# Cross attention on one core: block 2's first query projection moved in front of the first scores, and mask rows held until a block's maxima have landed

## What is computed

```python
q = split_heads(x @ W_Q.T); k = split_heads(ctx @ W_K.T); v = split_heads(ctx @ W_V.T)
scores = einsum('bhqd,bhkd->bhqk', q, k) / sqrt(16)
scores = where(mask[:, None, :, :] == 1, -1e9, scores)
p = softmax(scores, axis=-1)
concat = merge_heads(einsum('bhqk,bhkd->bhqd', p, v))
out = concat @ W_O.T + x                       # residual
out = (out - mean(out)) * rsqrt(var(out) + 1e-5) * gamma + beta
```

## Time and profile before

| what | value |
|---|---|
| device time, median of 3 runs | 176.94 us (175.6 to 178.7) |
| device time of the profiled execution | 177.09 us |
| its span from the first to the last instruction | 175.3 us |
| busy time of PE in the span | 152.7 us (87%) |
| busy time of DVE | 139.5 us (80%) |
| busy time of ACT | 105.1 us (60%) |
| busy time of POOL | 96.0 us (55%) |
| mean granted clock of TensorE | 0.971 of full speed |

### The profile page before, as it was taken

The page is one execution under the profiler, slowest core; times in us unless marked ns, Lnnn a source line. Parts: engine busy times, 40 slices in busy tenths (PEclk is TensorE's granted clock), DMA queues, the critical chain, the costliest instruction groups (busy, mean ns, idle before and its releaser), DMA issues.

```text
span 175.3 us, 3587 instructions
## 1 busy us (share of the span) xinstructions
PE 152.7 (87%) x1264; PEld 82.4 (47%) x1264; DVE 139.5 (80%) x308; ACT 105.1 (60%) x140; POOL 96.0 (55%) x125
## 2 busy tenths in 40 slices
PE   7699939887969999999999999998899798799840
PEld 7456515344335356345545544563456363164530
DVE  0967743569399969998999899899989975759894
ACT  3123224355377883888877897778576559796400
POOL 8300430010564525337767977974744785899890
PEclk9999985899999999999999999999999999999996
DMA  5959868764867997887498877749460023011206
GB/s 157 382 142 135 242 101 258 230 161 103 268 172 196 286 292 184 222 277 168 137 236 234 247 200 178 214 162 228 133 223 5 0 120 123 2 64 60 120 0 239
DMA packets 21909, 30.24 MB, mean 173 GB/s; under 512 B 3436, under 2 KB 17436, under 8 KB 21892
## 3 DMA queue, kind: packets, MB, share of 16 engines
q1 hardware_dynamic: 20340, 28.18, 56.4%
q10 hardware_dynamic: 1552, 1.84, 3.8%
HBM read 11.28 MB, written 4.19 MB: 88 GB/s over the span
## 4 chain that ended last, share of the span: by engine, by line
PE 51%; DVE 19%; DMA 10%; issue 9%; ACT 5%; POOL 2%; ACTq 1%; SPq 0%; DVEq 0%; POOLq 0%
PE pv_ps L993 12%; PE scores_ps L984 9%; DVE neg_max L725 7%; PE max_ps L951 6%; PE work_ps L924 6%; PE work_ps L930 5%; PE scores_ps L930 4%; DMA R<-neg_max_t 4%; DMA x_t<-in_x_cols 4%; DVE ctx_q L733 3%; PE work_ps L1012 3%; DMA R<-first_max_t 3%; ACT probs L594 2%; PE work_ps L1009 2%; ACT neg_max_t L584 1%
## 5 line engine op out<-in xcount | busy, mean ns | idle before, releaser
L594 ACT ACTIVATE probs<-scores_ps 78x1024 f32<-78x1024 f32 x60 | 60.5, 1016 | 24.4 <-PE scores_ps L984 19.6
L725 DVE TENSOR_REDUCE neg_max<-max_ps 128x6 f16<-128x462 f32 (+1 forms) x84 | 44.7, 560 | 5.2 <-PE max_ps L951 5.1
L951 PEld LDWEIGHTS max_ps<-kb,R 125*128 125x128 f16 x512 | 26.4, 99 | 36.9 <-DVE neg_max L725 21.0
L409 POOL TENSOR_TENSOR ctx_n<-ctx_q,rden 128x256 f32<-128x256 f32 x31 | 19.8, 639 | 43.0 <-DVE rden L735 42.9
L984 PE MATMUL scores_ps<-R,kb 127*78 127x512 f16 x120 | 37.0, 392 | 2.3 <-DMA R<-first_max_t 2.0
L951 PE MATMUL max_ps<-kb,R 125*128 125x77 f16 x512 | 32.5, 201 | 6.1 <-DVE neg_max L725 5.5
L993 PE MATMUL pv_ps<-probs,v_all 78*32 78x512 f32 x248 | 33.0, 604 | 2.6 <-ACT probs L594 1.5
L733 DVE STREAM_TRANSPOSE ctx_q<-pv_ps 128x512 f32<-128x512 f32 x31 | 21.8, 704 | 4.6 <-PE pv_ps L993 4.4
L430 POOL TENSOR_TENSOR y<-y,gamma_sb 128x512 f32<-128x512 f32 x14 | 17.8, 1276 | 2.4 <-ACT y L599 2.4
L392 POOL TENSOR_SCALAR eq<-mask_i 77x512 f16<-77x512 int32 x3 | 5.8, 1928 | 22.1 <-DMA mask_i<-in_mask_cols 22.1
L599 ACT ACTIVATE y<-y,shift,rstd 128x256 f32<-128x256 f32 x28 | 15.1, 591 | 3.6 <-POOL shift L423 3.6
(11 more groups left out here) (105 smaller groups left out, 198.7 us busy)
## 6 DMA issues: line engine op xcount, KB each, us to landing
R<-eq SPq DMA_DIRECT2D x12, 616.0 KB
R<-q SPq DMA_DIRECT2D x46, 128.0 KB
x_t<-in_x_cols SPq DMA_DIRECT2D x8, 512.0 KB, 5.9
y<-in_x SPq DMA_DIRECT2D x8, 512.0 KB, 6.0
out<-y SPq DMA_DIRECT2D x7, 512.0 KB, 2.7
mask_i<-in_mask_cols SPq DMA_DIRECT2D x8, 154.0 KB
out<-y ACTq DMA_DIRECT2D x2, 256.0 KB, 2.1
kb<-k SPq DMA_DIRECT2D x10, 39.0 KB, 3.2
```

Source lines behind the costliest of these rows:

```text
L409: nc.gpsimd.tensor_tensor(ctx_n[:, v, :, u * DK:(u + 1) * DK], ctx_q[:, t % 2, :, 0:DK], rden[:, t % 2, :].unsqueeze(2).to_broadcast([P, C ...
L594: nc.scalar.activation(probs[:, s, :, :], scores_ps[scores_buffer(PAIRS * n + s)[0]][0:COLS, :, :], ACT.Exp).then_inc(exp_done, 1)
L725: nc.vector.tensor_reduce(to[:, t, lo:hi], max_ps[u % 2][:, 0:(hi - lo) * KEYS].rearrange("p (h k) -> p h k", k=KEYS), AX.X, ALU.max, nega ...
L951: last = nc.tensor.matmul(max_ps[u % 2][:, (h - lo) * KEYS:(h - lo + 1) * KEYS], R[m % R_RING][0:MAX_ROW, h, t * P:(t + 1) * P], kb[0:MAX_ ...
```

## The change

Three things are edited.

1. `project_q(2, 0)` leaves step 1 of block 0 and goes in front of `scores(0, 0)`, behind the second `turn_first_max`. Its `q_hi` on ACT goes in front of `exp(0, 0)`, its `q_lo` on DVE behind `q_lo(1, 1)` and so in front of the reduction of unit 8.
2. On ACT `q_hi(3, 0)` no longer stands in step 6 behind `turn_max(1)`, but in step 5 in front of it.
3. On SP `load_q(n + 3, 0)` comes before `load_mask(n + 3, 0)`, and between them stands a new wait: the maxima of block n+1 must have landed.

```diff
@@ SP, loop over n
                 if n + 3 < N:
+                    load_q(n + 3, 0)
+                    sp.wait_ge(s_nm, 16 * (n + 1))
                     load_mask(n + 3, 0)
-                    load_q(n + 3, 0)
@@ ACT
             turn_first_max(1)
+            q_hi(2, 0, work_ps[:, :])
 
             for n in range(N):
                 for s in range(STEPS):
-                    if n == 0 and s in (4, 6):
-                        q_hi(2 + s // 6, s // 2 - 1 if s < 6 else 0, work_ps[:, :])
+                    if n == 0 and s == 4:
+                        q_hi(2, 1, work_ps[:, :])
...
                     exp(n, s)
                     if n == 0:
                         if s == 1:
-                            q_hi(2, 0, work_ps[:, :])
                             turn_first_max(2)
...
+                    if n == 0 and s == 5:
+                        q_hi(3, 0, work_ps[:, :])
                     if s == nm_at(n) and n + 1 < N:
                         turn_max(n + 1)
@@ DVE
             q_lo(1, 1, q_ps[1][1])
+            q_lo(2, 0, work_ps[:, :])
...
-                    if n == 0 and s in (2, 4, 6):
+                    if n == 0 and s in (4, 6):
                         q_lo(2 + s // 6, s // 2 - 1 if s < 6 else 0, work_ps[:, :])
@@ PE
             turn_first_max(1)
+            pe.wait_ge(v_ready, 2)
+            project_q(2, 0, work_ps[:, :])
             pe.wait_ge(q_low, HALVES)
             pe.wait_ge(s_last_rows, 64)
...
                     if n == 0:
-                        if s == 1:
-                            pe.wait_ge(v_ready, 2)
-                            project_q(2, 0, work_ps[:, :])
                         if s == 2:
```

## The result

The changed kernel took 185.47 us (median of 4, 183.72 to 186.63) against 177.21 us for the kernel before in the same measurements: a ratio of 1.046, 95% interval 1.040 to 1.053. It is slower, where 172.2 us was forecast. Medians here are over all executions, ratios leave out the disturbed ones. The profiled execution has a span of 184.0 us.

A forecast was written before the change was run, and what follows sets the result against it. TensorE, busy 152.7 of 175.3 us, was taken as the bound, with gains where it stands still or runs slowly. 3.65 + 1.0 + 0.28 = 4.9 us off 177.09 gave 172.2 us, range 171.0 to 175.6.

The forecast's parts named there:

- What bounds the kernel, and the places: TensorE's 2.01 us pause at 23.70 with half clock after it, its 1.57 us wait near 48, and 0.28 at 69.07.
- Edit 1, 3.65 us: Block 2's projection fills TensorE's pause at 23.70; first values start at 30.4 instead of 34.06, a gain of 3.65 us.
- Edit 2, 1.0 us: Block 3's query copy before block 1's maxima copy starts VectorE's transpose at 47.33 instead of 48.33, a gain of 1.0 us.
- The cover of 0.5 us: Under edit 2, block 1's maxima land at 50.6, scores want them at 51.1; worst landing would cost 2.2 us.
- Edit 3, "costs nothing and gives 0.28": Holding mask rows on SP removes block 2's 0.28 us wait for maxima at 69.07; later inputs keep cover, so no cost.
- So the shift stays: After the first values the old order follows, block 2's low part no longer on VectorE, so edit 1's 3.65 us is kept.
- late arrivals: Rival: block 1's maxima, block 4's inputs or the third group's maxima come late, costing 2.2 us; 174.4 us, chance 0.14.
- no effect: Rival: the edits do not reach the end; another chain, such as POOL's norm, holds the middle; 177 us, chance 0.08.
- The slower rival: Held mask rows delay `x_t` of blocks 5 to 7 and ACT stands in `x_hi`; 8.2 us more, 180.5 us, chance 0.06.
- The clock rival: The clock falls anyway, later, between 26 and 30.4, losing about 3.0 us of TensorE's work; 175.2 us, chance 0.12.
- The rule weighed against it: Issue DMAs early, wait late: by it edit 3's hold has no use and would lose at least its 0.28 us.

The follow-up runs named there:

- e1: Edits 1 and 2 without edit 3, SP's list as in the kernel before: 177.01 us, ratio 1.002 to the kernel before.
- e2: Edit 3 alone on the kernel before: 185.34 us, ratio 1.048.
- e4: The changed kernel with two buffers of `q16`, `q_hi` waiting for the rows of block m-2 instead of m-1: 176.37 us, ratio 0.999.
- e5: The changed kernel with query rows counted on their own semaphore, the only one `q_hi` waits for, one `q16` buffer: 183.2 us, ratio 1.036.
- e10: Edit 1 alone, `q_hi(3, 0)` staying in step 6, the rest as e1: 176.67 us, ratio 1.004 to the kernel before.
- e8: A second trace of edits 1 and 2 without the hold, the same kernel as e1: span 175.0 us.
- e6: e1 with 19 matmuls of zeros in two pauses of TensorE: 178.41 us, ratio 0.996 to the kernel before.
- e3: The changed kernel without its new wait, query rows still ahead of mask rows: 177.15 us, ratio 1.007 to the kernel before.
- e9: Edits 1 and 2 with e5's semaphore; SP issues query rows and inputs before the wait for maxima, mask rows after it: 180.31 us, ratio 1.022.

## Why the prediction was wrong

- *What bounds the kernel, and the places.* Right: the pause at 23.7 with its stretch at half clock, and VectorE's late start at 48.3.
- *Edit 1, 3.65 us.* Right in mechanism and size in this trace: first values at 30.63, 3.43 us earlier, with a program start 0.3 us later; the clock stayed up from 25 to 51.
- *Edit 2, 1.0 us.* Right for the gain, in this trace: the wait fell from 1.57 to 0.65 (0.6 forecast), the lead grew to 4.3 us. Block 1's scores didn't wait for their maxima in the changed kernel, but 0.90 us in e1. The cover of 0.5 us that I worked out was too thin; I had charged nothing.
- *Edit 3, "costs nothing and gives 0.28".* This step failed. I named as queued behind the new wait what stands behind it in SP's list, and priced the inputs of block n+4. I did not ask who waits for the held transfer itself. `q_hi` of the next block does, by a semaphore that counts mask rows and query rows together, and I had used this very wait once, for block 2, where the transfers had long landed. I had even put the second half's query rows at 2.9 us later and then followed only the inputs behind them. That they went out at 70.88, with 70.8 forecast, is luck: the maxima landed at 67.7 and not at 69.0, and the two mask issues took 3.1 us and not 1.8. The last of these rows, issued at 73.37, took 7.9 us to land. e2 gives the price, 4.8% of the time before (1.035 to 1.060); e4 shows that this one wait is the place, e5 that the mask rows counted in it are the smaller part and the query rows behind them the larger.
- *"So the shift stays", 4.65 us for edits 1 and 2.* This step failed as well, and the hold has no part in it: e1 took 1.002 of the time before, e10 1.004. The lead is won as forecast and then meets waits that weren't there, for maxima (0.90 and 0.76 us in e1) and for query rows (4.9 us of `q_hi` in e10). The size was also taken from one trace, of an execution that took 177.09 us, where later comparisons gave the kernel before medians of 176.0 to 177.45 us.
- *The rivals of late arrivals and of no effect* were given 0.14 and 0.08. The first describes e1 and e10 in part: block 1's maxima came late as written, but the query rows, which took the larger part in e10, are not in it. It was priced at 2.2 us; the lead shrank by 1.4 us in e1's trace (4.3 to 2.9) and by 3.0 in e10's. The second has e1's time (177 forecast, 177.01 measured) with a reason, POOL's norm, that no trace shows.
- *The slower rival* had the right sign for a wrong reason: in e4 the inputs were late by 8.8 us in total, more than the 8.2 us that it priced, and the time was that of the kernel before. (Its 8.2 should be 8.0 by its own numbers, 3 times 83.3 less 80.64.) Behind `q_hi` stand `q_lo`, the next projection into the single bank `work_ps` and the maxima's copy; that these make its wait the dearer one is my reading of the order, and no run separates it.
- *The clock rival* was given 0.12. It did not happen in the changed kernel's trace at that place, but it did in e8. The whole-program means say that it isn't rare: e1's executions have mean clocks from 0.959 to 0.990. But a full clock did not bring the gain: e1's four executions at 0.985 or more took 174.21 to 176.69 us, and in the comparison of e5 and e6 the kernel before had a median of 176.6 us in its ten executions at 0.985 or more and 176.3 us in its six from 0.974 to 0.985. So its price of 3.0 us is borne out by e8 beside e1 and not by these times.
- *The rule weighed against it.* The Trainium skill, "DMA: Bandwidth & Descriptors", section "Rules for kernel authors", says to issue DMAs early and wait late. I had left it at its 0.28 us. The runs side with it as the change was written (1.048 for the hold alone); where nothing needed soon stands behind the held rows they show no difference (0.996).

What stays open: what sets the moment at which the clock falls when edits 1 and 2 are in. Filling two pauses didn't prevent it, and no run here separates it from chance. How the missing gain of edits 1 and 2 divides over executions is not settled either: late transfers are enough in e10's trace, a stretch at half clock adds to them in e8's. Why the transfers land later when the program is ahead is not shown; from 51 to 85 us the transfer engines were busy for 0.78 of the time in the kernel before, 0.86 in e1 and 0.89 in e10. And no run has two `q16` buffers without the hold.

## What to carry to other kernels

Before a transfer is held back, list the waiters of its semaphore, not only the instructions behind it in its queue; a semaphore that counts several transfers makes every one of them wait for the latest. If a buffer's release is tied to such a count, give the readers of that buffer a count of their own or a second buffer first, and look at what the queue issues right behind the held transfers, since that lands late as well. And a lead won early in a program is worth only what the next wait leaves: here the landings of maxima and of query rows took it, in one trace with the help of the clock. A forecast in microseconds from one trace also needs the spread of that kernel's times beside it.

## What the runs showed of the hardware that I had not expected

The clock fell to half after pauses of quite different length: by 25.0 in the trace before, 1.3 us into a pause of 2.01 us, about 1 us after a pause of 2.42 us had ended at 76.7 in the changed kernel, and in e8 at about 31, behind a stretch from 25.6 in which TensorE was busy for 3.88 of 5.40 us. The same pauses in e1 left it at full speed. The landing of one small transfer, the 16 KB of maxima, took from 2.1 us to 7.0 us in e1 alone, and its median moved from 3.8 us before to 5.3 us in e1. The hold alone does not set it: the median was 3.1 us in the changed kernel and 5.2 us in e4, both with the hold, and 3.5 us in e3 without it. A transfer of 512 KB issued directly behind 1.2 MB of mask rows took 10.5 us to land in e9, against a median of 6.0 us for the same kind before.
